# Laying q and k out feature by feature, gathering them in three transfers each, and splitting the biases on a small tile

## The reference

```python
h = _layernorm(x) * (1 + ca) + sa
x = x + ga * _L0_attn_ref(h, ...)      # q, k, v, g projections with biases, rope, elu + 1,
                                       # chunked linear attention, gate, output projection
h = _layernorm(x) * (1 + cb) + sb
x = x + gb * _L0_ffn_ref(h, ...)       # 4-bit weights, gelu(gate) * up, down
h = _layernorm(x) * (1 + ca) + sa
x = x + ga * _L1_attn_ref(h, ...)      # causal softmax attention with biases and rope
h = _layernorm(x) * (1 + cb) + sb
x = x + gb * _L1_ffn_ref(h, ...)       # rmsnorm, a second causal softmax attention whose output
                                       # feeds a rank-16 term of the gate, silu(gate) * up, down
```

## Time and profile before

| | us |
|---|---|
| median of 3 runs (lowest, highest) | 713.77 (713.38, 720.05) |
| the profiled execution, its own time | 716.44 |
| its span, from first to last instruction | 714.7 |
| PE busy | 651.3 (91%) |
| DVE busy | 463.9 (65%) |
| ACT busy | 334.4 (47%) |
| POOL busy | 164.6 (23%) |

### The profile page before, as it was taken

One profiled execution on the slowest core, in us unless ns is written; L12 is line 12 of the kernel. 1 busy time (PEld: TensorE's weight loads), 2 busy tenths in 40 slices (PEclk: granted clock), 3 DMA queues, 4 the chain that ended last, 5 costly groups with the idle time before them and its releaser, 6 DMA issues.

```text
span 714.7 us, 10679 instructions
## 1 busy us (share of the span) xinstructions
PE 651.3 (91%) x3977; PEld 409.9 (57%) x3977; DVE 463.9 (65%) x970; ACT 334.4 (47%) x531; POOL 164.6 (23%) x200
## 2 busy tenths in 40 slices
PE   3699988999999979799999998888999999989996
PEld 3576746777777747444444434574554444368885
DVE  5868776777777388688988801656689887243223
ACT  3335143333333333336567685561555657843332
POOL 6601133555555431210000000030000001002231
PEclk9999599999999999899999999997999999999999
DMA  9502320000000001573000000037420000050001
GB/s 319 164 1 89 89 82 0 23 22 23 1 0 1 0 1 44 182 218 91 3 2 1 2 2 1 0 98 223 134 81 2 2 2 3 1 176 1 0 1 59
DMA packets 36335, 38.35 MB, mean 54 GB/s; under 512 B 3958, under 2 KB 35204, under 8 KB 36028
## 3 DMA queue, kind: packets, MB, share of 16 engines
q1 hardware_dynamic: 36284, 37.68, 16.7%
HBM read 30.13 MB, written 7.34 MB: 52 GB/s over the span
## 4 chain that ended last, share of the span: by engine, by line
PE 47%; issue 22%; POOL 12%; DVE 11%; ACT 3%; DMA 2%; SPq 2%; POOLq 0%; DVEq 0%; ACTq 0%
POOL it_lo L1601 9%; PE psum L777 9%; PE psum L737 8%; PE psum L763 8%; PE psum L452 3%; PE psum L454 3%; PE psum L453 3%; POOL wd L1580 2%; PE psum L495 2%; PE psum L566 2%; SPq L408 2%; PE psum L766 2%; PE psum L740 2%; DVE m L1280 2%; DVE stats L1103 1%
## 5 line engine op out<-in xcount | busy, mean ns | idle before, releaser
L957 ACT ACTIVATE pt<-psum 128x1024 f32<-128x1024 f32 (+1 forms) x192 | 148.0, 811 | 92.9 <-PE psum L766 64.7
L1280 DVE TENSOR_REDUCE mx<-psum 128x1 f32<-128x512 f32 (+3 forms) x216 | 132.4, 665 | 16.3 <-PE psum L737 8.3
L737 PE MATMUL psum<-kr,qr 96*128 96x512 bf16 (+3 forms) x384 | 111.0, 341 | 5.4 <-DMA kr<-parts_scratch 2.5
L1601 POOL TENSOR_TENSOR it_lo<-it,it_hi 128x512 fp32r<-128x512 f32 x48 | 67.3, 1401 | 153.6 <-ACT it_hi L1001 153.6
L763 PE MATMUL psum<-qr,kr 99*128 99x512 bf16 (+3 forms) x384 | 97.6, 327 | 1.5 <-ACT pt L957 1.3
L777 PE MATMUL psum<-pt,vp 128*32 128x512 f32 (+3 forms) x768 | 81.7, 498 | 0.0
L452 PE MATMUL psum<-h_hi,wf_hi 128*128 128x512 f32 x192 | 75.5, 393 | 1.7 <-issue 1.7
L737 PEld LDWEIGHTS psum<-kr,qr 96*128 96x128 bf16 x384 | 37.1, 100 | 67.5 <-DVE mx L1280 29.4
L453 PE MATMUL psum<-h_lo,wf_hi 128*128 128x512 f32 x192 | 75.0, 390 | 0.0
L454 PE MATMUL psum<-h_hi,wf_lo 128*128 128x512 f32 x192 | 74.9, 390 | 0.0
L1001 ACT CAST it_hi<-it 128x512 fp32r<-128x512 f32 x48 | 29.8, 622 | 95.7 <-DVE it L1355 95.7
(11 more groups left out here) (204 smaller groups left out, 1111.2 us busy)
## 6 DMA issues: line engine op xcount, KB each, us to landing
qr<-parts_scratch SPq DMA_DIRECT2D x48, 128.0 KB, 2.7
kr<-parts_scratch SPq DMA_DIRECT2D x48, 128.0 KB, 2.6
parts_scratch<-parts SPq DMA_DIRECT2D x12, 384.0 KB, 3.5
wmod<-in_L_wmod SPq DMA_DIRECT2D x1, 1536.0 KB, 6.1
parts_scratch<-qr SPq DMA_DIRECT2D x4, 384.0 KB, 3.3
x<-in_L_attn_x SPq DMA_DIRECT2D x2, 512.0 KB, 4.0
wmod<-in_L_wmod SPq DMA_DIRECT2D x1, 1024.0 KB, 7.2
packed<-in_L_ffn_gate_W_packed SPq DMA_DIRECT2D x1, 1024.0 KB, 9.2
```

Source lines behind the costliest of these rows:

```text
L737: m = pe.matmul(b, qr[0:PARTS_ROWS, c, h, (qt - 4 * c) * P:(qt - 4 * c + 1) * P], kr[0:PARTS_ROWS, ch, h, 0:w], start=True, stop=not diag)
L957: act.activation(pt[:, n % 4, :, 0:w], psum[:, b:b + 2, 0:w], ACT.Exp, scale=0.25).then_inc(S["ex"], 1)
L1280: dve.tensor_reduce(dst, bank[at[0]][:, 0:k * w].rearrange("p (k w) -> p k w", k=k), AX, ALU.max).then_inc(S["p1_mx"], 1)
L1601: pool.tensor_tensor(it_lo[:, N % 2, :], it[:, N % 2, :], it_hi[:, N % 2, :].bitcast(F32), ALU.subtract).then_inc(S["it_l"], 1)
```

## The change

- The weights' columns (and the biases) of q and k of both softmax attentions are permuted ahead of the launch, so that eight heads' values of one feature lie side by side: a run of 128 columns is feature major. DVE's rope of the second projection (L1178, L1190 before) reads and writes in that order.
- `parts_scratch` is laid out by piece, part, feature and token. A row of `qr` or `kr` is then one run of 8 heads x 512 tokens (8 KB) for a feature and a part. The six slots are filled as 3 + 2 + 1 slots of equal parts: for q a part is read three times, twice and once by a source with a repeat, for k three, two and one parts follow each other. A spread is six transfers of 48, 32 and 16 rows instead of twelve of 16 x 8 runs. q's reads wait for q's store alone and k's for k's.
- `rest` has four buffers instead of two, so L1218 waits for the last subtraction of w - 4.
- The biases are loaded as 12 rows of 128, split by four POOL instructions on 12 x 128, and moved by three transfers to three rows of `bias`; the product's other operand is `spin`, three rows of ones.
- ACT computes the silu ahead of the square root.
- `kr`'s rows of minus one are written in four quarters behind the last four POOL subtractions of `mlp(0)`. For that the overlaid tiles change place.
- `idle(9, 4)` is added behind the last transposes ahead of attention 0, and `idle(4, 3)` becomes `idle(8, 3)`.

```diff
-        rest = xn[:, 0:4, :].rearrange("p a b -> p (a b)").rearrange("p (c t) -> p c t", c=2)
+        rest = xn[:, :, :].rearrange("p a b -> p (a b)").rearrange("p (c t) -> p c t", c=4)
...
-        scr = nc.dram_tensor("parts_scratch", [4, P, 3, T], BF16, kind="Internal").ap()
+        scr = nc.dram_tensor("parts_scratch", [4, NH, 3, P, HALF], BF16, kind="Internal").ap()
...
+            load(brow[:, :], a["bias_rows"].rearrange("(c p) -> c p", p=P), "ld_bias")
...
-            sp.wait_ge(S["bias_z"], 1)
-            load(rb[0:P:32, 0:4 * D], a["bias_rows"][0:4 * D].partition_broadcast(4), "ld_bias")
...
+            sp.wait_ge(S["bias_s"], 4)
+            for i in range(3):
+                load(bias[i:i + 1, :], bpart[:, i, :], "bias_ok")
             load(wmod0[:, :, 512:1536], wm0[:, :, 512:1536], "ld_wmod0b")
...
-                    sp.dma_start(scr[w2, :, :, tok], piece(l, w2, half)).then_inc(S[f"pw{2 * half + dt}"], 16)
+                    sp.dma_start(scr[w2, half].rearrange("s p t -> p s t"), piece(l, w2, half)).then_inc(S[f"{'qk'[is_k]}w{2 * half + dt}"], 16)
 
             def spread(l, half, dt):
-                tok = slice(half * HALF, (half + 1) * HALF)
-                sp.wait_ge(S[f"pw{2 * half + dt}"], 32 * (l + 1))
-                for is_k, (dst, order) in enumerate([(qr, (0, 1, 0, 1, 0, 2)), (kr, (1, 1, 2, 2, 0, 1))]):
-                    for slot, part in enumerate(order):
-                        sp.dma_start(dst[slot:PARTS_ROWS:6, half, 8 * dt:8 * dt + 8, :],
-                                     scr[2 * dt + is_k, :, part, tok].rearrange("(h d) t -> d h t", d=DH)
-                                     ).then_inc(S[f"qr_ld{2 * half + dt}"], 16)
+                for is_k, dst in enumerate((qr, kr)):
+                    sp.wait_ge(S[f"{'qk'[is_k]}w{2 * half + dt}"], 16 * (l + 1))
+                    for part, (first, n) in enumerate(((0, 3), (3, 2), (5, 1))):
+                        src = scr[2 * dt + is_k, half].rearrange("s (d h) t -> s d (h t)", d=DH)
+                        if is_k:
+                            src = src[0:n]
+                        else:
+                            src = src[part:part + 1].to_broadcast([n, DH, 8 * HALF])
+                        sp.dma_start(dst[DH * first:DH * (first + n), half, 8 * dt:8 * dt + 8, :].rearrange("r h t -> r (h t)"),
+                                     src).then_inc(S[f"qr_ld{2 * half + dt}"], 16)
...
+            idle(9, 4)
...
                 if l == 0:
-                    idle(4, 3)
+                    idle(8, 3)
...
+            act.activation(silc[:, :, :], vec[:, 0:2, :], ACT.Silu).then_inc(S["silu_c"], 1)
             layer_norm_std(0)
-            act.activation(silc[:, :, :], vec[:, 0:2, :], ACT.Silu).then_inc(S["silu_c"], 1)
...
-                        if w >= 2:
-                            dve.wait_ge(*low_part(l, w - 2))
-                        dve.tensor_tensor(rest[:, w % 2, :], bank[w % 4][:, :],
+                        if w >= 4:
+                            dve.wait_ge(*low_part(l, w - 4))
+                        dve.tensor_tensor(rest[:, w % 4, :], bank[w % 4][:, :],
...
-            mlp(0)
-            pool.wait_ge(S["fdn"], 2 * FC[0])
-            pool.memset(kr[PARTS_ROWS:PARTS_ROWS + 3, :, :, :].bitcast(F32),
-                        float(np.array([0xBF80BF80], np.uint32).view(np.float32)[0])).then_inc(S["kr_ones"], 1)
```

More of the change, by code:

```diff
@@ L271, in build @@
         rb = sb("rb", [P, T])
-        bias = sb("bias", [P, 6 * D], BF16)
-        sel = sb("sel", [P, P], BF16)
+        brow = sb("brow", [12, P])
+        bpart = sb("bpart", [12, 3, P], BF16)
+        bias = sb("bias", [3, 6 * D], BF16)
         rope_c = sb("rope_c", [P, 2, NT, DH])
@@ L329, in build @@
             dq w_sc wf_h wf_l g_m u_m gl_s it_s it_h it_l fdn out_done""".split()
+        names += [f"{z}w{i}" for z in "qk" for i in range(4)]
         names += [f"nat{i}" for i in range(FC[1])] + [f"ld_scale{i}" for i in range(4)]
@@ L476, in token_major @@
                 if b0 is not None:
-                    pe.wait_ge(S["bias_ok"], 1 + b0 // T)
-                    m = pe.matmul(dst, sel[:, :], bias[:, b0:b0 + c1 - c0], start=False, stop=True)
+                    if b0 == 0 and t == 0:
+                        pe.wait_ge(S["spin_ok"], 1)
+                        pe.wait_ge(S["bias_ok"], 48)
+                    m = pe.matmul(dst, spin[0:3, 0:P], bias[:, b0:b0 + c1 - c0], start=False, stop=True)
                 return m
@@ L921, in middle @@
                     half, n = divmod(w, 4)
-                    act.copy(piece(l, n, half)[:, (1, 2)[n % 2], :], rest[:, w % 2, :]
+                    act.copy(piece(l, n, half)[:, (1, 2)[n % 2], :], rest[:, w % 4, :]
                              ).then_inc(S["sp_m"], 1)
@@ L1171, in pairs @@
                     return ap.rearrange("p (h j two) -> p h j two", h=2 * H, two=2)[:, :, :, i]
-                return ap.rearrange("p (h two j) -> p h two j", h=2 * H, two=2)[:, :, i, :]
+                return ap.rearrange("p (g two j h) -> p g two j h", g=4, two=2, h=8)[:, :, i, :, :]
             def rope_cos(l, t):
@@ L1223, in split @@
                         dve.wait_ge(S["sp_m"], 8 * l + w)
-                        dve.tensor_tensor(piece(l, n, half)[:, (2, 0)[n % 2], :], rest[:, (w - 1) % 2, :],
+                        dve.tensor_tensor(piece(l, n, half)[:, (2, 0)[n % 2], :], rest[:, (w - 1) % 4, :],
                                           piece(l, n, half)[:, (1, 2)[n % 2], :], ALU.subtract).then_inc(S["sp_l"], 1)
@@ L1538, in _ @@
             pool.memset(a_rep[:, :, :], 0.0).then_inc(S["a_rep_ok"], 1)
[L1540 to L1550, removed]
-                pool.wait_ge(S["bias_s"], 3 * i + 1)
-                pool.tensor_tensor(src[64:P], src[64:P], dst[64:P], ALU.subtract).then_inc(S["bias_s"], 1)
-                pool.wait_ge(S["bias_s"], 3 * i + 2)
-                pool.tensor_scalar(dst[64:P], src[64:P], 1.0, None, ALU.mult).then_inc(S["bias_s"], 1)
-                pool.wait_ge(S["bias_s"], 3 * i + 3)
-                pool.tensor_tensor(dst[96:P], src[96:P], dst[96:P], ALU.subtract).then_inc(S["bias_ok"], 1)
-            bias_parts(0, 4 * D)
-            bias_parts(1, 2 * D)
-            pool.wait_ge(S["bias_ok"], 2)
+            pool.wait_ge(S["ld_bias"], 16)
+            pool.tensor_scalar(bpart[:, 0, :], brow[:, :], 1.0, None, ALU.mult).then_inc(S["bias_s"], 1)
+            pool.wait_ge(S["bias_s"], 1)
+            pool.tensor_tensor(brow[:, :], brow[:, :], bpart[:, 0, :], ALU.subtract).then_inc(S["bias_s"], 1)
+            pool.wait_ge(S["bias_s"], 2)
+            pool.tensor_scalar(bpart[:, 1, :], brow[:, :], 1.0, None, ALU.mult).then_inc(S["bias_s"], 1)
+            pool.wait_ge(S["bias_s"], 3)
+            pool.tensor_tensor(bpart[:, 2, :], brow[:, :], bpart[:, 1, :], ALU.subtract).then_inc(S["bias_s"], 1)
+            pool.wait_ge(S["bias_s"], 4)
             pool.wait_ge(S["ld_a"], 16)
@@ L1615, in low_parts @@
                     pool.wait_ge(S["sp_m"], 8 * l + w + 1)
-                    pool.tensor_tensor(piece(l, n, half)[:, (2, 0)[n % 2], :], rest[:, w % 2, :],
+                    pool.tensor_tensor(piece(l, n, half)[:, (2, 0)[n % 2], :], rest[:, w % 4, :],
                                        piece(l, n, half)[:, (1, 2)[n % 2], :], ALU.subtract).then_inc(S["sp_p"], 1)
@@ L1691 @@
             inputs[n].reshape(FC[1], P, KC, P).transpose(0, 3, 2, 1).reshape(F1, D))
-    given["bias_rows"] = _np.concatenate([_np.array(inputs[n]) for n in (
-        "L0_attn_bq", "L0_attn_bk", "L0_attn_bv", "L0_attn_bg", "L1_attn_bq", "L1_attn_bk")])
+    spread = _np.arange(D).reshape(2, 8, DH).transpose(0, 2, 1).reshape(-1)
+    for n in ("L1_attn_Wq", "L1_attn_Wk", "L1_ffn_Wq", "L1_ffn_Wk"):
+        given[n] = _np.ascontiguousarray(given[n][:, spread])
+    given["bias_rows"] = _np.concatenate(
+        [_np.array(inputs[n]) for n in ("L0_attn_bq", "L0_attn_bk", "L0_attn_bv", "L0_attn_bg")]
+        + [_np.array(inputs[n])[spread] for n in ("L1_attn_bq", "L1_attn_bk")])
     for name, arr in [*given.items(), ("rope_cos", cos), ("rope_sin", sin)]:
```

69 lines of the change are left out of this document (42 added, 27 removed).

## The result

The change takes **768.33 us** (767.15 to 769.24), the kernel before 713.62 on the same chip: ratio 1.073, interval 1.069 to 1.078. It is slower by 55 us, where 14 were forecast. The profiled execution took 767.57 us, with a span of 765.8 where before had 714.7.

A forecast was written before the change was run, and what follows sets the result against it. PE bounds most stages, so the change counts only where PE stands still. Terms -6.9 - 0.6 + 0.1 + 2 x (9.8 + 1.0) = +14.2 on a median of 713.77 gave 728.0 us, range 715 to 737.

The forecast's parts named there:

- The start: Program start: earlier silu and POOL's smaller bias split let PE project near 18.1; -6.9 us, bounds -5 and -7.5.
- The third norm: Third norm: `ve` falls from 0.80 to about 0.17 us, -0.6; first quarter of the `kr` fill, +0.1.
- The bias products their 512 columns: 0: Bias products on PE: they keep their 512 columns, so their cost was put at 0.
- The number of engines: Spreads ahead of both attentions: q's 48- and 32-row transfers run on 3 and 2 engines, k's on 16.
- the first rival: Spreads run on all engines, 3.8 us each at 411 GB/s, giving 701.4 us; chance 0.13.
- 39 x 0.32 = 12.4 us: Each spread: engines 0 and 1 carry 39 packets of 8 KB at 0.32 us; 15.7 us between spreads, +9.8 per attention.
- +1 each: Each attention, behind block 1's wait: PE's work at the low clock adds 1 us (0 to 3).
- It decides at 29 to 33 packets: Packets on one engine per spread: at 29 the attentions lose nothing, at 33 they just eat the start's gain.
- the second rival: Row maxima do not queue behind the spread; only spread waits stay, +6 per attention, 718.4 us; chance 0.09.
- the deciding term: The spreads in both attentions: +9.8 us each, bounds +6.5 and +13.5 for each.
- the high end: Top of the forecast case's range: -5 + 0.6 + 27 + 2, near 738 us.
- within 1%: Outcome up to 720.9 us: the second rival and a twentieth of the forecast's case; chance 0.17.

The follow-up runs named there:

- e6: The kernel before with one edit, the silu ahead of the square root; one run, 716.1 us.
- e1: The change with all gathers of q and k walked with their 16 feature rows outermost, so on 16 engines; 711.15 us, ratio 0.994.
- e7: The change with only the 48-row gathers on 16 engines, q's 32-row gather staying on 2; 735.57 us, ratio 1.027.
- e4: The change with k's gathers left out and k's rows filled with a constant; one run, 738.57 us.
- e3: e1 plus bias products over 128 rows, zero but for the first three; 707.73 us, ratio 0.988.
- e5: e3 with the rows of one feature side by side again, so target rows 6 apart, four transfers each for q and k; 704.75 us, ratio 0.984.
- e8: Control for e5: the same four transfers each, but into neighbouring rows as in e3; one run, 710.1 us.

## Why the prediction was wrong

It had the mechanism, the direction and the places, and the time was outside its range: 768.33 against 728.0 (715 to 737). In the spans it is 51.1 against 14.2, 36.9 short. In the order of its parts:

- **The start, -6.9:** measured -7.4 (PE at 17.54 for 18.1). `onep` takes 0.17 us, two `h_lo` 1.29, as said. PE waits for no bias. e6 splits the gain, about 4.2 and 3.2.
- **The third norm, -0.6 and +0.1:** right. `ve` takes 0.17 us, the quarters 1.80 each, and PE's waits for POOL's `it_lo` stay at 7.2 us (7.1 before).
- **"The bias products their 512 columns: 0":** wrong. 24 products at 0.28 us, **6.7 us**, 16 in the first projection, 8 in the second. I priced the instruction by its columns and not the break it makes in a stream of overlapping products. Of these, 2.0 came back between the two projections by PE waiting less or running longer at 1.00 of its clock there; which, no experiment separates (the granted clock from 84 to 93 us is 1.00 with the change and 0.70 before). With the start it leaves -2.9 where the forecast had -7.4: 4.5 of the 36.9.
- **The number of engines:** right: 3, 2 and 16 engines (the counts of small packets in the change, e1 and e7), the same ones for all, with the stores and the row maxima in line behind them (the landing of 18.1 us, the wait of 6.8, the share of 0.10 to 0.18). No row shows which numbers they have. The Trainium skill's rule for the number of engines ("DMA: Bandwidth & Descriptors"), cited in the forecast, agrees with 39, 26 and 12 packets; its advice to join small transfers, the first rival, gave a kernel no slower than before only with rows walked as in e1.
- **"39 x 0.32 = 12.4 us":** the step that failed. 16.9 to 18.6 us from the first packet to the last, 0.46 us for each of the 39 in the first spread. The 0.32 came from loads at the start, which fill all partitions, and I bounded it from there by a tenth. Those were the wrong rows: no transfer of before moves 8 KB rows into few partitions. What it missed is that the engines slow each other. 39 packets at 0.31 are 12.1 us, so 6.0 of the 18.1 are to be explained: 2.1 of them need k's gathers, and 3.9 are there with q's alone (e4). With all engines at work a packet takes 0.5 to 0.8 us, and with three left two of them can still take 0.6; 0.31 holds only at the end. The rest of the step was nearly right. It had store 1.1, receipt 0.8 and start 1.4, and the first spread shows 1.0, 0.4 and 1.5, with the stores behind the spread as forecast. So it is 21.1 us from spread to spread, not 15.7. At block 1's first score PE has lost 23.5 us since the stores of attention 0 and 23.2 since those of attention 1, not 9.8: **27.1 of the 36.9**.
- **"+1 each" for what follows the waits:** from that score on another 3.5 and 3.8 us are lost, to make 27.0; forecast as 1 in each, within a bound of 3; this is the other 5.3 of the 36.9. 0.5 us of each is a further wait for a row maximum. PE's granted clock is 0.62 in the stretch of the wait shown above, and the first products behind it take 0.61 us instead of 0.38. How the rest divides wasn't tried.
- **The rivals.** The first, all engines, 701.4: the wide version e3 is 707.7, and e5, with far rows, 704.75. Its 3.8 us for a spread at 411 GB/s was wrong for the same reason, and attention 1 kept 1.5 us of its waits in e3. "It decides at 29 to 33 packets" was too kind: 26 already cost 10 to 13 us an attention. The second, row maxima that don't queue, is out: PE waits 6.8 us for one.

The range was too narrow because both bounds of the deciding term were taken from one row and its neighbours, and that row's load differed from the change's in the one thing that mattered. Two of its sums were off as well, and neither would have saved it: the high end took 1 us for each attention where its own bound was 3 (742, not 738), and the second rival's 0.09 and a twentieth of 0.76 make 0.13 for "within 1%", not 0.17.

## What to carry to other kernels

Put an axis of 16 (or a multiple) slowest on both sides of every transfer, repeats inside it, and let the target rows of one transfer spread over the partitions: the same bytes took 16.9 to 18.6 us with neither, 8.9 to 10.1 with the first, and 6.4 to 7.2 with both. The price of a packet depends on the rows it is written to and on what the other engines do meanwhile; a transfer with another target needs its own row, or bounds a factor of two wide. And a matmul on few rows amid full ones is not free: its cost lies in the starts of its neighbours, not in its duration.

## What the runs showed of the hardware

- A DMA share near 1.0 is no rate: 138, 181 and 259 GB/s at shares of 0.99 to 1.01 in e8, e3 and e5, against 411 for the loads at the start, by the rows that are written.
- A transfer on 2 or 3 engines delays every later one on the queue: stores of 384 KB landed in 18.1 us, in 9.2 (e1) and in 4.0 (e5).
- A bf16 product on 3 rows between products on 128 costs 0.28 us beyond its duration, at a granted clock of 1.00.
